# Recurrent attention phase of a two-layer kernel: the gate rows of chunk 0 made, stored and spread first, and the instruction orders of four engines written out per batch

## The chip, the cores and the metric

One core of one Trainium2 chip runs the whole program in one launch. The metric is the device time in microseconds (us) of a run, of which the median over some runs is given. The engines are called PE (matrix products), ACT (activations, copies with a scale), DVE (elementwise and scans), POOL (GpSimd) and SP (which issues DMAs).

## What is computed

The reference has two layers. The change concerns only the attention of layer 0, a gated recurrent attention (mLSTM) over 4 batches of 512 positions, 256 channels and 8 heads:

```python
logfg = jax.nn.log_sigmoid(f_pre)                 # gates, capped by 15 * tanh(x / 15)
Fcum = jnp.cumsum(logfg, axis=-1)
Dmat = Fcum[..., :, None] - Fcum[..., None, :] + i_pre[..., None, :]
Dmat = jnp.where(causal, Dmat, -jnp.inf)
m = jnp.max(Dmat, axis=-1, keepdims=True)
Smat = jnp.exp(Dmat - m)
C = qk * Smat
n = jnp.maximum(jnp.abs(jnp.sum(C, axis=-1, keepdims=True)), jnp.exp(-m))
h = jnp.einsum('bhst,bhtd->bhsd', C / n, v)
...
x1 = x + (jax.nn.sigmoid(o_pre) * h_norm) @ w_out
```

After it come the MLP of layer 0 with a mixture of low-rank experts, and layer 1 with softmax attention and a sparsified MLP. Those phases fill the time from about 140 us on.

## The kernel before

The attention phase is `mlstm_phase`. The 512 positions of a batch b are cut into C = 4 chunks of P = 128, so there are N = 16 chunks n = 4b + c. Every engine has its own list of instructions, executed in order, with semaphore waits between engines. A matrix product in full precision is three PE passes (`product`, lines 94 to 96) over operands split in a high and a low part: ACT copies the high part, DVE subtracts to get the low part.

**The gate rows.** After `gates(b)` has put the gate preactivations of all batches in one bank, ACT and DVE make rows of 32 x 512 (batch and head by position): ACT `Tanh`, `Exp`, `Tanh` and `Ln` (lines 745 to 750), DVE `gate_rows` (lines 1058 to 1078): a combination, a scan for the running sum `Fcum` (`F_SUM`, line 1068), a combination (line 1070), and a scan for the running maximum (`G_ROW`, line 1072). SP then stores the row in DRAM (`m_scratch`, line 361) and, for each chunk, loads it back spread over all 128 partitions (`spread_rows`, line 358) into one of a ring of six tiles `W`, 512 KB each. PE turns the gates (`turn_gates`, `TG_T`) and spreads sums (`spread_decay`), which ACT copies out or exponentiates (`tg`, `ends`, `ea`, and `eq` by `decay_of_queries`).

**A chunk n.** POOL masks W (`mask_weights`, line 849), ACT turns it to weights by eight `Exp` (`weights`, line 710), PE makes the scores (`score`, line 492) in banks 0 to 3, DVE multiplies scores and weights (`weigh_scores`, line 980, signals `PT_ready`), PE forms the weighted sum (`weighted`, lines 519 and 524) and the local state (`local_state`, line 507), DVE carries the state (`carry`), ACT evicts (`evict`, lines 717 and 718, "m_tot" and "m_sq"). `score(n)` waits for `weigh_scores(n - 1)`, since the banks are single.

**A batch b.** PE makes k, q, v and the output gate (`project_k`, `project_q`, `project_v`, `output_gate`) and ACT copies them out (lines 677, 682, 688, 693, 701). The results are normed in two halves f of two chunks: `mean_square`, `sum_squares` on DVE, `inverse_root` on POOL (line 863), `gate` and `norm` on DVE, `turn_h` on PE, `high_h` on ACT (line 731), `low_h` on DVE, `project_out` on PE, `add` on DVE. The order around the chunks is a loop `for b in range(B - 1)` with a body per engine, the same for b = 0, 1 and 2, and a written-out end for b = 3.

**The hand-over.** `following` is the opening of the next phase: squares of the result of batch 0 (`squares`, line 1317), their root on POOL, `scale_y` (line 1335), `turn_y` on PE, `high_y` and `low_y`, splits of the MLP weights (`split_high`, `split_low`), then `gates(pe, 0)` and `gates(pe, 1)`, the first two MLP units on PE, and `silu` and `hidden` for unit 0. Behind them the next phase puts its third unit on PE.

## Time and profile before

| | |
|---|---|
| median of 3 runs | 693.9 us (693.79 to 694.63) |
| the profiled execution's own time | 692.77 us |
| its span in the trace | 690.9 us |
| PE, DVE, ACT, POOL busy | 97%, 75%, 54%, 19% of the span |
| TensorE clock granted over the span | 0.998 of full |

A span is the time from the first to the last instruction of the trace; the execution's own time is 1.9 us more. Positions such as "at 40.17" are us from the start of the span. "Busy" of PE counts modelled ends of pipelined products, so a gap that the trace shows on PE is a lower bound of the time in which it had nothing to do.

### The profile page before, as it was taken

How to read it: one execution, taken by the hardware profiler on the slowest of the kernel's cores; microseconds unless marked ns; L12 is line 12 of the kernel's file. 1: busy time of each engine (PE TensorE's matmuls, PEld its weight loads, DVE VectorE, ACT ScalarE, POOL GpSimd, SP SyncE). 2: the span in 40 equal slices, each digit the busy share in tenths (PEclk: the TensorE clock that was granted, in tenths of full speed). 3: DMA queues.
4: the chain of work that ended last, by engine and by line, in shares of the span. 5: the costliest groups of instructions: out<-in, count | busy, mean ns of one | idle time of the engine just before them, and what ended most of it. 6: DMA issues, size and time to landing. Idle time of an engine off the chain costs nothing.

```text
span 690.9 us, 12153 instructions
## 1 busy us (share of the span) xinstructions
PE 666.7 (97%) x4808; PEld 560.5 (81%) x4808; DVE 518.5 (75%) x919; ACT 371.5 (54%) x775; POOL 129.3 (19%) x125
## 2 busy tenths in 40 slices
PE   7989998999999999999999999999899999999996
PEld 7867886878787888878888788887787889889886
DVE  7837879868856667565765676757679998989996
ACT  5887888747543444434443443446565454464541
POOL 7145445300000020000200002000133303203220
PEclk9999999999999999999999999999999999999999
DMA  5088442000210002000010100240000000000000
GB/s 198 5 264 313 108 146 71 1 1 1 63 29 4 1 1 64 1 31 1 1 64 0 32 1 1 93 183 2 0 1 1 0 17 16 1 31 1 1 31 31
DMA packets 24008, 31.27 MB, mean 45 GB/s; under 512 B 1232, under 2 KB 19952, under 8 KB 23184
## 3 DMA queue, kind: packets, MB, share of 16 engines
q1 hardware_dynamic: 23296, 29.18, 12.9%
q10 hardware_dynamic: 656, 1.31, 0.5%
q8 instruction: 38, 0.62, 0.4%
q14 instruction: 18, 0.15, 0.1%
HBM read 28.18 MB, written 2.31 MB: 44 GB/s over the span
## 4 chain that ended last, share of the span: by engine, by line
PE 62%; DVE 22%; ACT 9%; issue 3%; DMA 2%; POOL 1%; SPq 0%; DVEq 0%; ACTq 0%; POOLq 0%
PE bank L94 20%; PE bank L96 19%; PE bank L95 19%; ACT m_W L710 3%; DVE l_ring_lo L2551 3%; DVE l_ge L2532 2%; DVE l_h L2547 2%; DVE l_o L2555 1%; DVE h_raw L1227 1%; DVE l_h L2504 1%; DMA res<-in_x 1%; DVE h_ring_lo L1232 1%; DMA m_W<-m_scratch 1%; PE bank L519 1%; DVE l_oT_lo L2561 1%
## 5 line engine op out<-in xcount | busy, mean ns | idle before, releaser
L1227 DVE TENSOR_TENSOR h_raw<-h_s,bank 128x512 f32<-128x512 f32 x104 | 71.4, 686 | 107.1 <-ACT h_s L1217 92.7
L1217 ACT ACTIVATE h_s<-bank 128x512 f32<-128x512 f32 x104 | 62.2, 598 | 164.6 <-PE bank L96 164.5
L1232 DVE TENSOR_TENSOR h_ring_lo<-h_raw,h_ring_hi 128x512 fp32r<-128x512 f32 x92 | 68.9, 749 | 0.1
L1221 ACT ACTIVATE h_ring_hi<-h_raw 128x512 fp32r<-128x512 f32 x104 | 64.7, 623 | 2.0 <-DVE h_raw L1227 2.0
L95 PE MATMUL bank<-fused_lo,h_ring_hi 128*128 128x256 f32 x208 | 58.4, 281 | 0.0
L2251 ACT ACTIVATE l_s<-bank 128x512 f32<-128x512 f32 x32 | 19.1, 598 | 62.8 <-PE bank L96 62.6
L94 PE MATMUL bank<-l_xT_hi,l_wgu 128*128 128x512 f32 x128 | 51.2, 400 | 0.3
L94 PE MATMUL bank<-f_yT_hi,mlp_hi 128*128 128x512 f32 x128 | 50.6, 396 | 0.0
L95 PE MATMUL bank<-l_xT_lo,l_wgu 128*128 128x512 f32 x128 | 50.0, 391 | 0.0
L96 PE MATMUL bank<-l_xT_hi,l_lo 128*128 128x512 f32 x128 | 50.0, 390 | 0.0
L96 PE MATMUL bank<-f_yT_hi,fused_lo 128*128 128x512 f32 x128 | 50.0, 390 | 0.0
L95 PE MATMUL bank<-f_yT_lo,mlp_hi 128*128 128x512 f32 x128 | 49.9, 390 | 0.0
L94 PE MATMUL bank<-f_xT_hi,ffn_hi 128*128 128x512 f32 x104 | 41.5, 399 | 0.5 <-DVE h_raw L1227 0.5
L96 PE MATMUL bank<-f_xT_hi,fused_lo 128*128 128x512 f32 x104 | 40.7, 391 | 0.0
L95 PE MATMUL bank<-f_xT_lo,ffn_hi 128*128 128x512 f32 x104 | 40.6, 390 | 0.0
L95 PEld LDWEIGHTS bank<-fused_lo,h_ring_hi 128*128 128x128 f32 x208 | 39.2, 189 | 1.4
L710 ACT ACTIVATE m_W<-m_W,m_tg 128x128 f32<-128x128 f32 x128 | 39.2, 409 | 1.2 <-POOL m_W L849 1.2
L1729 POOL TENSOR_TENSOR late_rstd<-f_vv,minus_half 128x4 f32<-128x4 f32 x3 | 3.0, 1011 | 187.5 <-DVE f_vv L1878 187.5
L94 PE MATMUL bank<-l_wd,l_ring_hi 128*128 128x256 f32 x128 | 36.1, 282 | 1.6 <-DVE l_ring_lo L2551 1.6
L94 PE MATMUL bank<-mlp_hi,h_ring_hi 128*128 128x256 f32 x128 | 35.9, 281 | 0.7 <-DVE h_ring_lo L1232 0.7
L96 PE MATMUL bank<-mlp_hi,h_ring_lo 128*128 128x256 f32 x128 | 35.8, 280 | 0.0
L95 PE MATMUL bank<-l_lo,l_ring_hi 128*128 128x256 f32 x128 | 35.7, 279 | 0.0
(372 smaller groups left out, 1970.5 us busy)
## 6 DMA issues: line engine op xcount, KB each, us to landing
m_W<-m_scratch SPq DMA_DIRECT2D x16, 512.0 KB, 6.9
fused_raw<-in_fused SPq DMA_DIRECT2D x1, 3584.0 KB, 12.6
res<-in_x SPq DMA_DIRECT2D x4, 512.0 KB, 6.1
fused_raw<-in_fused SPq DMA_DIRECT2D x2, 1024.0 KB, 9.1
f_mask<-expert_weights SPq DMA_DIRECT2D x8, 256.0 KB
l_raw<-in_layer SPq DMA_DIRECT2D x1, 2048.0 KB, 8.9
out_x<-res SPq DMA_DIRECT2D x16, 128.0 KB, 1.9
f_xw<-in_turned_x SPq DMA_DIRECT2D x3, 512.0 KB, 5.7
```

The source lines that it names most:

```text
L94: nc.tensor.matmul(out, w[0], x[0], start=start, stop=False, skip_group_check=True)
L95: nc.tensor.matmul(out, w[0], x[1], start=False, stop=False, skip_group_check=True)
L96: return nc.tensor.matmul(out, w[1], x[0], start=False, stop=stop, skip_group_check=True)
L710: last = nc.scalar.activation(w[:, h, :], w[:, h, :], ACT.Exp, bias=tg[:, c, b * H + h:b * H + h + 1], scale=-1.0)
L1217: self.nc.scalar.activation(self.s[u % 2][r, :], gate[r, :], ACT.Silu).then_inc(self.silu.sem, 1)
L1221: self.nc.scalar.activation(self.unit(i, u)[0], self.product(i, u), ACT.Copy).then_inc(self.hi.sem, 1)
L1227: self.nc.vector.tensor_tensor(out=self.product(i, u), in0=self.s[u % 2][r, :], in1=up[r, :], op=ALU.mult).then_inc(self.hidden.sem, 1)
L1232: self.nc.vector.tensor_tensor(out=lo, in0=self.product(i, u), in1=f32(hi), op=ALU.subtract).then_inc(self.lo.sem, 1)
L2251: nc.scalar.activation(sb[u % 2][:, :], gate(u)[:, :], ACT.Silu).then_inc(silu.sem, 1)
L2532: nc.vector.tensor_tensor(out=ge[:, at:at + n, :], in0=ab[:, x, :].unsqueeze(1).to_broadcast([P, n, S]), in1=ab[:, x + 1:GP, :], op=ALU.is ...
L2547: nc.vector.scalar_tensor_tensor(out=x, in0=votes[:, j, :], scalar=least, in1=x, op0=how, op1=ALU.mult).then_inc(kept.sem, 1)
L2551: nc.vector.tensor_tensor(out=ring[j][1][:, :], in0=h[c][j][:, :], in1=f32(ring[j][0][:, :]), op=ALU.subtract).then_inc(lo.sem, 1)
```

## The change

**Gate rows in two parts.** `Ln`, the two combinations and the two scans run first on the 128 columns of chunk 0 and then on the other 384, the second scans starting from the last value of the first. SP stores chunk 0's part and spreads it at once; the rest is stored when `G_ROW` is there, and the other five tiles of the ring follow. In DRAM the rows lie as (chunk, row, position), so that a partition's 8 heads are one run of 4096 bytes where they were eight of 512. ACT also copies k of batch 0 between two of the row operations.

**Banks and waits.** The sums spread by PE go to banks 7, 4, 7, 4 and 4, so that banks 0 to 3 are free for `score(0)`, which now waits for `tg` and `x_rows` alone. ACT makes the weights of chunk 0 ahead of the decays.

**Orders written out.** The loops over b on PE, ACT, POOL and DVE become flat lists in which each batch has an order of its own; around the hand-over the squares and some splits stand elsewhere.

```diff
-    scratch = nc.dram_tensor("m_scratch", (R, S), fp32, kind="Internal").ap()
+    scratch = nc.dram_tensor("m_scratch", (C, R, P), fp32, kind="Internal").ap()
-    tg_bank, small_bank, spread_banks = bank[0], bank[1], [bank[2], bank[3], bank[4], bank[4]]
+    tg_bank, small_bank, spread_banks = bank[0], bank[4], [bank[7], bank[4], bank[7], bank[4]]
+    parts = slice(0, P), slice(P, S)
@@ sync
-            rows = scratch[of(b), chunk(c)].unsqueeze(0).to_broadcast([P, H, P])
-            sp.dma_start(W[n % RING][:, :, :], rows).then_inc(loaded[n % RING], 16)
-        sp.wait_ge(dve_rows, G_ROW)
-        sp.dma_start(scratch, row[5][0:R, :]).then_inc(stored, 16)
+            rows = scratch[c, of(b), :].rearrange("h s -> (h s)").unsqueeze(0).to_broadcast([P, H * P])
+            sp.dma_start(W[n % RING][:, :, :].rearrange("p h s -> p (h s)"), rows).then_inc(loaded[n % RING], 16)
+        sp.wait_ge(dve_rows, G_HEAD)
+        sp.dma_start(scratch[0], row[5][0:R, 0:P]).then_inc(stored, 16)
         sp.wait_ge(stored, 16)
         sp.wait_ge(gated, 1)
-        for n in range(RING):
+        spread_rows(0)
+        sp.wait_ge(dve_rows, G_ROW)
+        sp.dma_start(scratch[1:C].rearrange("c r s -> r c s"), row[5][0:R, P:S].rearrange("r (c s) -> r c s", s=P)).then_inc(stored, 16)
+        sp.wait_ge(stored, 32)
+        for n in range(1, RING):
             spread_rows(n)
@@ tensor
         def spread_decay(b):
-            if b == B - 1:
-                pe.wait_ge(eq_ready.sem, eq_ready.at(b - 1, 1))
+            if b == 0:
+                pe.wait_ge(og_in.sem, og_in.at(0, 2))
+            elif b == 1:
+                pe.wait_ge(act_tables, ENDS_IN)
+            else:
+                pe.wait_ge(eq_ready.sem, eq_ready.at(b - 2, 1))
@@ score(0)
-                pe.wait_ge(eq_ready.sem, eq_ready.at(1, 1))
-                pe.wait_ge(act_tables, ENDS_IN)
+                pe.wait_ge(act_tables, TG_IN)
+                pe.wait_ge(rows_in, 1)
@@ scalar
         nc.scalar.activation(row[1][f, :], row[0][f, :], ACT.Exp, scale=-CAP).then_inc(act_rows, 1)
+        copy_k(0)
         nc.scalar.activation(row[4][f, :], row[0][f, :], ACT.Tanh, scale=0.5 * CAP).then_inc(act_rows, 1)
         act.wait_ge(dve_rows, Y1)
-        nc.scalar.activation(row[3][f, :], row[2][f, :], ACT.Ln).then_inc(act_rows, 1)
+        for part in parts:
+            nc.scalar.activation(row[3][f, part], row[2][f, part], ACT.Ln).then_inc(act_rows, 1)
@@ vector, gate_rows
+            for p, ln, soft, f_sum, a_row, before in ((parts[0], LN_HEAD, SOFT1_HEAD, F_HEAD, A_HEAD, None),
+                                                      (parts[1], LN, SOFT1, F_SUM, A_ROW, slice(P - 1, P))):
...
+                nc.vector.tensor_tensor_scan(out=row[5][i, p], data0=gr[0:R, p], data1=gr[0:R, p], initial=row[5][i, before] if before else -3e38,
+                                             op0=ALU.max, op1=ALU.max).then_inc(dve_rows, 1)
@@ tensor, order of batch 0 (batches 1 to 3 have lists of their own)
+        local_state(0, 0)
+        score(1)
+        weighted(0, 0)
+        project_v(1, 0)
+        score(2)
+        weighted(0, 1)
+        project_v(1, 1)
+        local_state(0, 1)
+        score(3)
+        weighted(0, 2)
+        local_state(0, 2)
+        output_gate(1, 0)
+        score(4)
+        turn_h(0, 0)
+        output_gate(1, 1)
+        weighted(0, 3)
+        project_out(0, 0)
```

On DVE, in `gate_rows` from the `Ln` to the maximum, the kernel before has these rows (numbers behind the names are buffer numbers):

```order
L1066 SCALAR_TENSOR_TENSOR m_row_109<-m_row_109,m_row_111 32x512
L1068 SCALAR_TENSOR_TENSOR m_row_110<-ones_row,m_row_109 32x512
L1070 SCALAR_TENSOR_TENSOR m_gr<-m_row_108,m_row_110 32x512
L1072 SCALAR_TENSOR_TENSOR m_row_113<-m_gr 32x512
L1075 TENSOR_TENSOR m_qrow<-m_row_113 32x384
```

and the changed kernel these:

```order
L1151 SCALAR_TENSOR_TENSOR m_row_109<-m_row_109,m_row_111 32x128
L1153 SCALAR_TENSOR_TENSOR m_row_110<-ones_row,m_row_109 32x128
L1156 SCALAR_TENSOR_TENSOR m_gr<-m_row_108,m_row_110 32x128
L1158 SCALAR_TENSOR_TENSOR m_row_113<-m_gr 32x128
L1151 SCALAR_TENSOR_TENSOR m_row_109<-m_row_109,m_row_111 32x384
L1153 SCALAR_TENSOR_TENSOR m_row_110<-ones_row,m_row_110,m_row_109 32x384
L1156 SCALAR_TENSOR_TENSOR m_gr<-m_row_108,m_row_110 32x384
L1158 SCALAR_TENSOR_TENSOR m_row_113<-m_gr,m_row_113 32x384
```

Four rows of 512 columns became four of 128, after which chunk 0 can be stored, and four of 384.

On ACT, between the gate tables and the weights of chunk 1, the kernel before has these rows ("m_W_141" is the ring tile of chunk 0, "m_W_142" that of chunk 1):

```order
L769 ACTIVATE m_ea<-m_tg 128x128
L772 ACTIVATE m_eq<-bank 128x384
L776 ACTIVATE m_dexp<-m_dec 128x12
L772 ACTIVATE m_eq<-bank 128x384
L779 ACTIVATE m_ea<-m_ga 128x128
L772 ACTIVATE m_eq<-bank 128x384
L710 ACTIVATE m_W_141<-m_W_141,m_tg 128x128 x8
L677 ACTIVATE m_kT_105<-bank 128x512
L710 ACTIVATE m_W_142<-m_W_142,m_tg 128x128 x8
```

and the changed kernel these:

```order
L818 ACTIVATE m_ea<-m_tg 128x128
L753 ACTIVATE m_W_141<-m_W_141,m_tg 128x128 x8
L813 ACTIVATE m_eq<-bank 128x384
L720 ACTIVATE m_kT_105<-bank 128x512
L813 ACTIVATE m_eq<-bank 128x384
L824 ACTIVATE m_dexp<-m_dec 128x12
L826 ACTIVATE m_ea<-m_ga 128x128
L813 ACTIVATE m_eq<-bank 128x384
L753 ACTIVATE m_W_142<-m_W_142,m_tg 128x128 x8
```

The weights of chunk 0 moved ahead of five small operations, which now stand between the weights of chunks 0 and 1.

On ACT, at the end of the phase, the kernel before has these rows ("m_W_144" is the weights of chunk 15, "f_junk" the squares, "f_ys" is `scale_y`):

```order
L710 ACTIVATE m_W_144<-m_W_144,m_tg 128x128 x8
L717 ACTIVATE m_tot<-bank 128x264
L718 ACTIVATE m_sq<-bank 128x256
L1317 ACTIVATE f_junk_83,y_sq<-xn 128x256 x4
L731 ACTIVATE m_hT_hi<-bank,cols 128x256 x2
L140 ACTIVATE mlp_hi<-fused_raw 128x512 x2
L717 ACTIVATE m_tot<-bank 128x264
L718 ACTIVATE m_sq<-bank 128x256
L1335 ACTIVATE f_ys_82<-xn,y_rs 128x256 x4
```

and the changed kernel has the squares earlier, between two output gates of batch 3 ("m_th_145"):

```order
L744 ACTIVATE m_th_145<-bank 128x512
L1429 ACTIVATE f_junk_83,y_sq<-xn 128x256 x4
L774 ACTIVATE m_hT_hi<-bank,cols 128x256 x2
L744 ACTIVATE m_th_145<-bank 128x512
L760 ACTIVATE m_tot<-bank 128x264
L761 ACTIVATE m_sq<-bank 128x256
L753 ACTIVATE m_W_142<-m_W_142,m_tg 128x128 x8
```

The four squares moved from behind the weights of chunk 15 to ahead of those of chunk 13. Further on, `silu` of unit 0 ("h_s") moved behind the four copies "xn" and the last `high_h`, and two splits of MLP weights moved ahead of the last eviction.

## Rows read from the trace of the kernel before

**Rows 1.** The page: busy time, share of the span and instructions of each engine.

```profile
PE 666.7 (97%) x4808; PEld 560.5 (81%) x4808; DVE 518.5 (75%) x919; ACT 371.5 (54%) x775; POOL 129.3 (19%) x125
```

**Rows 2.** Stretches: length, then PE, PEld, DVE, ACT, POOL busy; clock, DMA share, GB/s.

```profile
40.00:60.00 20.00, 17.26 (x318) 13.40 (x322) 11.74 (x22) 18.10 (x58) 9.64 (x8) 1.00 0.95 326
60.00:68.00 8.00, 7.73 (x114) 5.46 (x105) 6.50 (x11) 4.77 (x15) 5.79 (x4) 1.00 0.83 272
68.00:90.00 22.00, 21.88 (x394) 17.92 (x394) 17.61 (x34) 17.47 (x54) 11.17 (x8) 1.00 0.43 118
90.00:112.00 22.00, 21.07 (x455) 17.05 (x457) 17.03 (x35) 19.40 (x61) 10.84 (x8) 1.00 0.45 146
112.00:124.50 12.50, 10.05 (x246) 7.20 (x241) 11.63 (x27) 11.09 (x35) 6.74 (x4) 1.00 0.01 3
124.50:140.00 15.50, 15.49 (x91) 13.76 (x92) 13.85 (x31) 12.64 (x26) 4.55 (x3) 1.00 0.01 2
```

**Rows 3.** The chain that ended last, 27 to 40 us: start, duration, what.

```profile
27.39 0.64 ACT m_row L750
...
28.12 0.69 DVE m_row L1066
...
28.84 1.22 DVE m_row L1068
...
32.04 1.63 DMA m_scratch<-m_row
...
33.68 5.22 DMA m_W<-m_scratch
...
39.05 1.10 POOL m_W L849
```

**Rows 4.** Timeline of ACT, 26 to 43 us: start, duration, instruction, [idle before, releaser].

```profile
26.09 1.28 ACT L750 ACT_TABLE_LOAD   x1
...
37.14 0.49 ACT L772 ACTIVATE m_eq<-bank 128x384 f32<-128x384 f32 x1 [0.26 <-PE bank L478]
...
40.17 2.45 ACT L710 ACTIVATE m_W<-m_W,m_tg 128x128 f32<-128x128 f32 x8 [1.25 <-POOL m_W L849]
```

**Rows 5.** Timeline of DVE, at 33 us.

```profile
33.33 0.28 DVE L1078 TENSOR_TENSOR m_diag<-ident,m_row 32x128 f32<-32x128 f32 x1
```

**Rows 6.** Line 351, the four loads of x, 4096 bytes per partition each.

```profile
DMA to landing us min/median/max: 4.0/6.1/8.8
```

**Rows 7.** Timeline of ACT, 57 to 68 us.

```profile
57.62 0.39 ACT L717 ACTIVATE m_tot<-bank 128x264 f32<-128x264 f32 x1 [0.52 <-PE bank L524]
...
59.49 0.60 ACT L701 ACTIVATE m_th<-bank 128x512 f32<-128x512 f32 x1 [1.20 <-PE bank L96]
...
61.27 0.39 ACT L717 ACTIVATE m_tot<-bank 128x264 f32<-128x264 f32 x1 [0.45 <-PE bank L524]
...
65.72 0.60 ACT L677 ACTIVATE m_kT<-bank 128x512 f32<-128x512 f32 x1 [1.46 <-PE bank L96]
...
67.64 1.27 ACT L682 ACTIVATE m_q<-bank,odd_even 128x512 f32<-128x512 f32 x2 [1.32 <-PE bank L96]
```

**Rows 8.** Timeline of ACT, 105 to 118 us.

```profile
105.06 0.60 ACT L701 ACTIVATE m_th<-bank 128x512 f32<-128x512 f32 x1 [1.21 <-PE bank L96]
...
106.83 0.39 ACT L717 ACTIVATE m_tot<-bank 128x264 f32<-128x264 f32 x1 [0.45 <-PE bank L524]
...
115.46 0.43 ACT L1317 ACTIVATE f_junk<-xn 128x256 f32<-128x256 f32 x1
...
117.51 0.82 ACT L731 ACTIVATE m_hT_hi<-bank,cols 128x256 fp32r<-128x256 f32 x2
```

**Rows 9.** Timeline of the hand-over: scale_y, silu of unit 0, third unit on PE.

```profile
119.80 1.71 ACT L1335 ACTIVATE f_ys<-xn,y_rs 128x256 f32<-128x256 f32 x4
...
127.54 0.60 ACT L1217 ACTIVATE h_s<-bank 128x512 f32<-128x512 f32 x1 [0.76 <-PE bank L96]
...
133.36 0.40 PE L94 MATMUL bank<-f_yT_hi,mlp_hi 128*128 128x512 f32 x1
```

More of the change, by code:

```diff
@@ new lines, in _ @@
+        score(7)
+        output_gate(2, 0)
+        weighted(1, 2)
+        output_gate(2, 1)
+        turn_h(1, 0)
+        weighted(1, 3)
+        score(8)
+        local_state(2, 0)
+        project_out(1, 0)
+        project_k(3)
+        score(9)
+        project_q(3)
+        weighted(2, 0)
+        score(10)
+        turn_k(3)
+        local_state(2, 1)
+        turn_h(1, 1)
+        weighted(2, 1)
+        project_v(3, 0)
+        project_v(3, 1)
+        weighted(2, 2)
+        local_state(2, 2)
@@ new lines, in _ @@
+        weights(6)
+        evict(1, 0)
+        high_h(0, 1)
+        copy_values(2, 0)
+        evict(1, 1)
+        weights(7)
+        copy_values(2, 1)
+        weights(8)
+        output_gate(2, 0)
+        evict(1, 2)
+        output_gate(2, 1)
+        high_h(1, 0)
+        evict(1, 3)
+        weights(9)
+        weights(10)
+        copy_k(3)
+        copy_q(3)
+        evict(2, 0)
+        copy_keys(3)
+        high_h(1, 1)
+        evict(2, 1)
+        weights(11)
+        copy_values(3, 0)
@@ L1133, in _ @@
[L1133 to L1151 removed]
+        weigh_scores(1)
@@ new lines, in _ @@
+        gate(0, 1)
+        weigh_q(2)
+        norm(0, 1)
+        carry(1, 0)
+        weigh_scores(5)
+        low_h(0, 1)
+        following.hid.credit_hidden(dve)
+        carry(1, 1)
+        mean_square(1, 0)
+        weigh_scores(6)
+        add(0, 1)
+        sum_squares(1, 0)
+        gate(1, 0)
+        weigh_scores(7)
+        carry(1, 2)
+        norm(1, 0)
+        normal_x(1)
+        low_h(1, 0)
+        mean_square(1, 1)
+        weigh_scores(8)
+        sum_squares(1, 1)
+        add(1, 0)
@@ new lines, in _ @@
+        gate(1, 1)
+        weigh_scores(9)
+        norm(1, 1)
+        carry(2, 0)
+        weigh_q(3)
+        normal_x(2)
+        low_h(1, 1)
+        weigh_scores(10)
+        mean_square(2, 0)
+        carry(2, 1)
+        gate(2, 0)
+        sum_squares(2, 0)
+        weigh_scores(11)
+        carry(2, 2)
+        norm(2, 0)
+        add(1, 1)
+        low_h(2, 0)
+        following.mean_square(dve)
+        weigh_scores(12)
+        mean_square(2, 1)
+        sum_squares(2, 1)
+        carry(3, 0)
```

396 lines of the change are left out of this document (193 added, 203 removed).

## The prediction

> **What bounds the kernel now.** I first read the busy line of the page [rows 1]: PE is busy 97% of the span, so over the whole program only a gap on PE can be won, and there are 690.9 - 666.7 = 24 us of them that the trace shows. Then I cut the span in stretches and looked for the gaps [rows 2]. From 124.5 to 140 us PE is busy 15.49 of 15.5 us: from the hand-over on, the rest of the program follows PE, and whatever is won before simply moves it forward. Ahead of it there are three kinds of stretch. From 40 to 60 us PE is short of work (17.26 of 20) while ACT is nearly full (18.10): ACT is the bound of batch 0. From 60 to 112 us PE is nearly full (7.73 of 8, 21.88 of 22, 21.07 of 22). From 112 to 124.5 us PE is short again (10.05 of 12.5), with ACT at 11.09 and DVE at 11.63. The PE gaps that the trace shows from 40 to 124.5 us add up to 2.74 + 0.27 + 0.12 + 0.93 + 2.45 = 6.5 us. The gaps are a lower bound, since the end of a product is modelled.
>
> Third, the chain that ended last shows what starts ACT's stretch [rows 3]: Ln, the combination, the scans, then the store of the gate row (1.63 us), the spreading load (5.22) and the mask on POOL (1.10), all in series, until ACT can make the first weights at 40.17. The timeline of ACT has 0.26 and 1.25 us of idle time just ahead of them [rows 4], and later, in the second half of batch 0, five waits for PE of 0.52, 1.20, 0.45, 1.46 and 1.32 us, 4.95 together [rows 7]. So ACT and PE take turns in waiting for each other.
>
> **Chunk 0 first.** ACT copies k ahead of the second Tanh, which puts about 0.5 us (0.60 in [rows 7], of which 0.1 overlaps) before the table load of 1.28 [rows 4]. Ln on 128 columns then starts at 27.4 + 0.5 = 27.9. Its price is not in the trace; it lies between a quarter of 0.64 [rows 3] and the 2.45 / 8 = 0.31 of an ACT operation with 128 columns [rows 4], and I take 0.3, as that has the same length: 28.2. On DVE two combinations of 128 columns cost 0.28 each [rows 5], and two scans, 1.22 for 512 columns [rows 3], between 0.28 and 0.31 by the column; I take 0.33 with overhead. With a gap of 0.03 us behind each that is 1.35 us, so chunk 0's row is ready at 29.6 instead of 32.0. The store takes 1.63 again: 31.2. The load has 128 runs of 4096 bytes instead of 1024 of 512. Its price is bounded by the 5.22 of before and by the 4.0 us of the fastest load of x, of the same size and the same runs [rows 6]. It lands between 35.2 and 36.4, and the mask and its start cost 1.2: W of chunk 0 is ready between 36.4 and 37.6.
>
> The Trainium skill's page "DMA: Bandwidth & Descriptors", section Specifications, gives 512 bytes as the smallest transfer at line rate, by which longer runs would win nothing and the load would stay at 5.22. By that the first weights start at 37.6, by the row of x at 36.9. I take 37.2, so this rule decides 0.4 us at most.
>
> The tables tg and ea are ready at about 36.9 as before (the operation ahead of the 37.14 row), for the longer part of the gate rows is split off: eight DVE instructions for four put the last scan some 0.6 us later, at 32.6, and what follows on PE waits for the second output gate anyway. So the first weights start near 37.2, 3 us earlier; but the 1.8 us of small ACT operations that filled 36.9 to 40.2 now stand behind them. The gain on ACT is the idle time alone: 1.51 less 0.3 = **1.2 us**. The other five spreads queue behind the second store, at about 34.3, 0.6 us later than the first one left before; the weights of chunk 1 are wanted only at 41.3, so this is hidden by the 4.1 us of ACT work ahead of them (2.3 of weights and the 1.8), as the load lands by 39.5 and the mask is done by 40.7. If the cover were gone, each us would count on ACT.
>
> **The order of batch 0.** The same instructions stand in another order, so the price is only in waits. Of the 4.95 us that ACT waits in [rows 7], the new lists put `high_h` and an eviction in front of the second output gate, which was the wait of 1.20, and score(0) and the projections no longer wait for the decays. Both engines must be free for a gain: PE shows 3.0 us of gaps from 40 to 68, ACT 1.5 + 4.95 = 6.5 us of waits. Going through the two new lists, I find one new wait of about 1 us, that of the last eviction of batch 0 for weighted(0, 3), which now stands behind the second output gate on PE; behind that eviction ACT has the gate copy and the weights of chunk 5. I take **3.5 us** for the head and batch 0 together, between 3.0 (the gaps shown) and 5.0 (half of the hidden part too).
>
> **Batches 1 and 2.** PE is nearly full; it shows 0.12 + 0.93 us of gaps from 68 to 112. I take **0.5 us**, between -0.5 (a wait more) and 2.
>
> **The end.** The squares take ACT 117.51 - 115.46 = 2.05 us [rows 8], in the middle of a stretch where ACT has no idle time from 106.83 on. They move to a place where ACT waited for PE 1.21 and 0.45 us [rows 8], which hides 1.7 of the 2.05. The end can follow only as far as DVE does: it is busy 11.63 of 12.5 us there [rows 2], but has 5 us free in the stretch ahead (17.03 of 22). I take **1.4 us**, between 0.5 and 2.4 (the gaps of PE).
>
> **The hand-over.** Silu of unit 0 came 127.54 - 119.80 = 7.7 us behind the start of `scale_y`, and PE's third unit, which needs its banks, 13.6 us behind [rows 9]. Now silu has more ahead of it. By the column, from 0.60 for 512, 1.71 for four times 256 and 0.82 for twice 256 [rows 7 to 9], I price scale_y at 1.7, the splits of 1536 columns at 1.5, high_y 1.2, the eviction 0.6, high_h 0.8, the four copies of x 1.7, the last two high_h 1.0, and the table load is 1.28: about 9.8 us, and with silu (0.5) and the product on DVE (0.6, a guess from the same 512 columns) 10.9. The slack is 2.7 us, so I count 0.2 for small waits of DVE, which is 13.85 of 15.5 us busy.
>
> The table load is 1.28 us in the row, and the copy behind it follows without more [rows 3, 4]. The Trainium skill's page "ScalarE: Activation LUTs", section What ACT_TABLE_LOAD costs, adds a drain of 1.38 for 2.66 together. By the page the slack would be 1.3 us; the sum is the same either way.
>
> The sum is 3.5 + 0.5 + 1.4 - 0.2 = 5.2 us: a span of 685.7, an own time of 692.8 - 5.2 = 687.6 us. The profiled execution was 1.1 below the median of its runs, so against that median I predict 693.9 - 5.2 = **688.7 us**.
>
> **The rivals.**
>
> *Only the head counts.* The middle is PE's and the end is DVE's: in 112 to 124.5 DVE leaves 0.9 us, and a batch that starts earlier only waits longer there. For it speaks the DVE row, against it that DVE is busy only 17.6 of 22 and 17.0 of 22 ahead, so it would be early as well. Then 1.2 of the head and 0.3 of the end remain: 692.4 us.
>
> *The hidden gaps go too.* PE's shown gaps are a lower bound, and ACT's waits are 6.5 us in the head alone. If the lists fit well, 4.7 us come in the head, 1.5 in the middle and 2.0 at the end: 8.2 less, 685.7 us. For it: no engine is full over 40 to 112 us but PE, whose busy time is overstated. Against it: fixed orders seldom hit both engines.
>
> *Order against the clock: slower.* In the new lists PE's output gates and v products stand directly ahead of a weighted sum or a score, and each waits for ACT to empty its bank. Where ACT is late, PE stops, and ACT then waits for PE: one round costs what such a wait costs now, 1.2 to 1.5 us [rows 7]. There are four such places a batch, twelve in all. The saving of 5.2 is gone with the fourth that newly bites; with six of the twelve the time is 6 x 1.35 - 5.2 = 2.9 above: 696.8 us. My walk through batch 0 found one.
>
> *The change does nothing.* The load of chunk 0 doesn't come earlier since 128 partitions read the same 4096 bytes, say 3 us more, and the small waits eat the rest: 693.9 us. The DMA engines are 0.95 busy from 40 to 60 us [rows 2] but idle before 34, so little speaks for it.
>
> **How the numbers follow.** A measurement of this kernel tells some 0.2%, or 1.4 us, from no change. Chances: forecast 0.55, with a range of its own from 686.5 to 691; only the head 0.15; hidden gaps 0.13; does nothing 0.08; slower 0.09. Only the head lies at the edge, a third of it within 0.2%. So faster 0.55 + 0.13 + 0.10 = 0.78, the same 0.13, slower 0.09. The range runs from 684.8, below the hidden gaps, to 693.5, beyond the head alone: it leaves out the slower case, half of no change and a little below, under 0.2 in all.
>
> **What would show it.** The first weights on ACT near 37.2 instead of 40.17, with the load of chunk 0 at 4.0 to 5.2 us. ACT without a gap of 1.2 us from there to the second output gate of batch 1. The weights of chunk 6, at 69.3 before by the ACT work behind the last of [rows 7], near 65.8. The squares ahead of the weights of chunk 13, and no ACT gap behind them. The first MLP product, at 124.5 before, near 119, and PE full from there; the third unit 8.9 us behind it. I am wrong if PE shows new waits on ACT's copies of v or the gates, if the third unit comes later than that by more than 0.5 us, or if the gain at 68 us has melted by 112.

## The result, and the profile after

The changed kernel takes 695.65 us (median of 12, 693.64 to 698.06), the kernel before beside it 693.76 (692.48 to 694.63): a ratio of 1.0026, with an interval from 1.0014 to 1.0039. It is slower by 0.26%, a small loss but clear of the interval, where 688.7 us were forecast with a range from 684.8 to 693.5. The profiled execution's own time is 695.59 us, its span 693.8, its granted clock 0.993 (before 692.77, 690.9 and 0.998).

The busy line of the page barely moved [rows 1]:

```profile
PE 668.6 (96%) x4808; PEld 561.5 (81%) x4808; DVE 521.5 (75%) x923; ACT 371.9 (54%) x776; POOL 130.1 (19%) x125
```

The stretches of [rows 2] in the kernel after (length, then PE, PEld, DVE, ACT, POOL busy, clock, DMA share, GB/s):

```profile
40.00:60.00 20.00, 16.99 (x273) 12.31 (x272) 9.04 (x17) 16.62 (x55) 9.32 (x7) 0.91 0.95 349
60.00:68.00 8.00, 7.91 (x120) 6.69 (x118) 6.91 (x13) 4.76 (x15) 3.40 (x3) 1.00 0.39 110
68.00:90.00 22.00, 20.92 (x387) 16.56 (x386) 18.26 (x34) 18.65 (x59) 12.01 (x7) 1.00 0.43 152
90.00:112.00 22.00, 21.89 (x396) 17.44 (x394) 17.08 (x35) 18.25 (x57) 11.50 (x7) 1.00 0.36 124
112.00:124.50 12.50, 10.59 (x308) 7.13 (x306) 11.87 (x29) 11.75 (x38) 6.52 (x3) 1.00 0.15 58
```

From 40 to 60 us PE has less work done than before at a clock of 0.91, and ACT, which was full, has 1.5 us less. Two places explain it. The first is the start of the program; the chain that ended last begins in the kernel after with

```profile
1.25 5.63 DMA gate_bias<-in_bias
...
6.90 0.15 DVE gate_bias L1169
...
7.04 1.32 DVE m_st L1024 x4
```

Here stands an edit that the forecast never priced and that the section on the change doesn't name: the line that scales `gate_bias` by 1/CAP, and its wait for two small loads, moved ahead of `statistics(0)`. In the kernel before the statistics start at 4.83 us; now they start at 7.0, and with them all that follows (the first gate product at 18.6 instead of 16.3). PE has nothing to do meanwhile, and the windows behind show its clock at the lower of its two levels, 1.2 GHz, for longer:

```profile
10.00:12.00 2.00, 0.00 (x0) 0.00 (x0) 1.93 (x12) 1.59 (x4) 1.18 (x3) 0.90 0.88 356
12.00:14.00 2.00, 1.46 (x7) 1.46 (x8) 1.93 (x12) 2.00 (x5) 1.15 (x3) 0.50 0.05 18
14.00:16.00 2.00, 1.93 (x10) 1.53 (x9) 1.93 (x11) 2.00 (x5) 1.14 (x3) 0.50 0.00 0
16.00:18.00 2.00, 2.00 (x11) 2.00 (x10) 1.98 (x3) 2.00 (x4) 1.92 (x4) 0.50 0.00 0
```

Before, the same windows have 1.00, 0.66, 0.50 and 0.98. The second place is in the chain near 50 us, inside `weighted(0, 1)`:

```profile
49.80 0.33 PE bank L527 x24
50.13 2.51 issue
52.64 0.78 PE bank L527 x40
```

and in the windows and the timeline of ACT around it:

```profile
50.00:52.00 2.00, 0.13 (x17) 0.02 (x3) 1.19 (x1) 1.25 (x5) 0.14 (x1) 1.00 1.05 442
52.00:54.00 2.00, 1.36 (x42) 1.20 (x43) 0.03 (x1) 0.00 (x0) 0.00 (x0) 0.64 1.07 459
54.00:56.00 2.00, 2.00 (x10) 1.90 (x9) 0.67 (x2) 1.37 (x5) 0.00 (x0) 0.51 0.84 363
```

```profile
54.63 0.39 ACT L760 ACTIVATE m_tot<-bank 128x264 f32<-128x264 f32 x1 [3.38 <-PE bank L532]
...
61.74 0.60 ACT L744 ACTIVATE m_th<-bank 128x512 f32<-128x512 f32 x1 [1.24 <-PE bank L96]
```

PE stops behind product 24 of 64 without waiting for any data ("issue"), then runs some 3 us at about half its clock, and ACT waits 3.38 us for it. The rest is as the change meant it. The SP timeline and the first weights:

```profile
32.11 0.34 SPq L363 DMA_DIRECT2D m_scratch<-m_row  x1
34.02 0.34 SPq L360 DMA_DIRECT2D m_W<-m_scratch  x1
...
37.75 2.48 SPq L360 DMA_DIRECT2D m_W<-m_scratch  x5
...
43.81 0.36 SPq L112 DMA_DIRECT2D fused_raw<-in_fused  x1
```

```profile
39.11 2.44 ACT L753 ACTIVATE m_W<-m_W,m_tg 128x128 f32<-128x128 f32 x8
```

The load of chunk 0 takes 3.7 us from its issue to the mask at 37.71 (5.4 before, [rows 3]). The last row of SP is new too: five spreads are issued in 2.48 us, so the first load of the fused weights, 3.5 MB, starts at 43.81, where the kernel before starts it at 46.92.

The signs that the forecast named came out like this. The first weights on ACT start at 39.11 us (forecast 37.2), those of chunk 6 at 71.89 (65.8), the first MLP product at 127.94 (119), and the third unit 9.0 us behind that (8.9).

All versions have the same number of products behind them at the weights of chunk 9 (977), at those of chunk 15 (1467) and at the first MLP product (1704), so the span can be cut there. The cuts, from the timelines of DVE, ACT and PE, in us:

| | before | after | e4 |
|---|---|---|---|
| start to the first statistics | 4.83 | 6.97 | 4.92 |
| to the weights of chunk 0 | 35.34 | 32.14 | 32.07 |
| to the weights of chunk 9 | 44.71 | 48.73 | 45.07 |
| to the weights of chunk 15 | 27.71 | 28.95 | 28.97 |
| to the first MLP product | 11.92 | 11.15 | 10.69 |
| to the end | 566.34 | 565.89 | 565.69 |
| span | 690.85 | 693.83 | 687.41 |

(Version e4 is the changed kernel with two edits undone, below. The traces of before and of e4 are of executions about 1 us faster than their medians, that of after is not.) Against before, the changed kernel gains 3.2 us in the head, 0.8 at the end and 0.4 behind it, and pays 2.1 at the start, 4.0 in batch 0 and 1.2 in batches 1 and 2.

Executions of one kernel differ by their mean granted clock: of 145 of the kernel before, 75 had 0.997 or more and a median of 693.0 us, the others 694.7, and below "at a full clock" is the median of the first kind.

### The profile page after: what moved, and what is told of

It reads as the page before. It is cut to its first block, busy times and chain, and to the rows that moved or that the text cites. A ratio compares the mean times of both kernels' runs of the same rounds, so it can differ in the third digit from the quotient of the medians.

```text
span 693.8 us, 12159 instructions
## 1 busy us (share of the span) xinstructions
PE 668.6 (96%) x4808; PEld 561.5 (81%) x4808; DVE 521.5 (75%) x923; ACT 371.9 (54%) x776; POOL 130.1 (19%) x125
## 4 chain that ended last, share of the span: by engine, by line
PE 70%; DVE 20%; ACT 5%; issue 3%; POOL 1%; DMA 1%; ACTq 0%; DVEq 0%
PE bank L94 22%; PE bank L96 20%; PE bank L95 20%; DVE l_ring_lo L2663 3%; DVE l_ge L2644 2%; DVE l_h L2659 2%; DVE l_o L2667 1%; PE bank L527 1%; DVE l_h L2616 1%; PE bank L500 1%; DVE h_raw L1339 1%; PE bank L532 1%; DVE xn L1128 1%; DMA gate_bias<-in_bias 1%; PE bank L515 1%
```

## The experiments

Medians are of 12 executions, of 6 for e4 and e15, 11 for e9. A ratio is to the kernel before on the same chip. The experiments ran on five chips (e1 to e4; e5 to e8; e9 to e12; e13 to e15; e16 and e17), on which the kernel before had medians from 693.24 to 694.15 us, so a difference of medians across chips is uncertain by some 0.9 us. Figures at a full clock compare only a part of the executions, and the part differs from kernel to kernel, so both are given where they disagree. Each version has one trace.

**e1: the bias line back.** On DVE:

```diff
-        dve.wait_ge(cols_loaded, 32)
-        nc.vector.tensor_scalar(out=gate_bias15..., scalar1=1.0 / CAP, ...)
         for b in range(B):
             statistics(b)
+        dve.wait_ge(cols_loaded, 32)
+        nc.vector.tensor_scalar(out=gate_bias15..., scalar1=1.0 / CAP, ...)
```

> The changed kernel with one line put back: DVE scales the gate bias behind the statistics of x, as in the kernel before, and not ahead of them. Theory A (DVE waits at that line for the small load of the bias, which lands at 6.9 us, while x is there at 4.8; all that follows is 2.0 to 2.3 us late): the first statistics start at 4.8 instead of 7.0, the first gate product on PE at 16.3 instead of 18.6, and the median falls by 2.0 us against the changed kernel, to about 693.7. Rival (the start is hidden, since PE waits for the projection weights or the store of the gate rows anyway): less than 0.5 us. If the stop of PE at 50 us hangs on where the big load of weights meets PE's code, it may move as well.

**e2: the kernel before with the bias line at the front** (the same edit the other way round).

> The kernel before with that one line moved to the front of DVE, as the changed kernel has it. Theory A: 2.0 us slower than the kernel before, about 695.8, with the first statistics at 7.0. Rival: below 0.5 us slower.

e1 took 693.03 us, 2.6 less than the changed kernel, ratio 0.9981 (0.9964 to 0.9998); e2 696.31, ratio 1.0032 (1.0018 to 1.0046), 2.2 more than the kernel before there. Its chain starts with the same wait (5.89 us of "DMA gate_bias<-in_bias"). None of the 12 executions of the changed kernel and none of e2 had a full clock, 7 of 12 of e1. So the line costs 2.2 to 2.6 us. The rest of the change wins 1.1 us over the kernel before there, and not 5: the stop is there in e1 too, 3.06 us at 48.6.

**e3: the load in small pieces.** e1, with the first fused load as seven of 1024 columns (4096 bytes a partition instead of 28,672):

```diff
-[[(g.fused_raw[:, a:b], fused_in[:, a:b])] for a, b in zip(cuts, cuts[1:])]
+the first group as [(g.fused_raw[:, n:n + 1024], fused_in[:, n:n + 1024]) for n in range(a, b, 1024)]
```

> As the kernel with the bias line put back, and the first load of fused weights (3584 KB in rows of 28672 bytes) cut into seven loads of 4096 bytes per partition. Theory B (PE stopped for 2.5 us at 50 us in the middle of a weighted sum because its next block of code waited on a DMA engine behind packets of 28672 bytes, 1.06 us each; the stop then halved the TensorE clock for some 3 us): with packets of 4096 bytes the stop shrinks to under 0.5 us, the granted clock stays at 1.0 from 50 to 58 us, and the time falls by 2.5 to 4 us against the kernel with the bias line put back. Rival C (PE waits there for something of its own, a semaphore or a bank, that the trace does not name): the stop stays at 2.5 us at the same instruction.

693.36 us, ratio 0.9984 (0.9969 to 1.0), and a stop of 2.23 us at the same product. The theory expected under 0.5 us; the size of the load's pieces isn't the cause.

**e4: the load later.** e1, with

```diff
-        after.issue(sp, 0)
         for n in range(RING, N):
             spread_rows(n)
+            if n == 7:
+                after.issue(sp, 0)
```

> As the kernel with the bias line put back, and the first load of fused weights issued behind the spreading load of chunk 7 instead of ahead of that of chunk 6, some 5 to 8 us later. Theory B: no stop in the weighted sum at about 48 to 50 us, but the code blocks that PE fetches every 6 us can meet the load later, so a stop of 1 to 2.5 us may show elsewhere; 0 to 4 us faster than with the bias line alone. Rival C: the stop stays at the same instruction, and the time changes by less than 0.5 us.

690.09 us, ratio 0.9932 (0.9918 to 0.9947). The stop is gone, the windows from 46 to 58 us are all at 1.00. It is 4.1 us faster than the kernel before there, at the upper end of what was expected. As **e15** it ran again on another chip, as the measure for e13 and e14:

> The kernel of e4 once more, as the measure for e13 and e14 on their chip: 690.0 to 690.4 us at a full clock, ratio to before between 0.993 and 0.996. If its six executions were a lucky sample the ratio is above 0.997.

689.94 us, 0.9947 (0.9933 to 0.9961). The gain holds.

**e5: the same edit in the kernel before; e9: the same edit in the changed kernel** with its bias line still at the front.

> The kernel before with one edit: its first load of the fused weights is issued behind the spread of chunk 7 instead of ahead of that of chunk 6. The trace of the kernel before has no stop of PE near 50 us. Theory (the late load in e4 won because it no longer lies ahead of PE's instruction block): there is nothing to win here, so within 0.1% of before, 693.5 to 694.9, first MLP unit within 0.5 us of 124.5. Rival (a late load is worth its 4 us by itself, since chunk loads or splits come sooner): 690 to 691, ratio near 0.994.

> The changed kernel with one edit: the first load of the fused weights is issued behind the spread of chunk 7; the line of gate_bias15 stays at the very front of DVE. If the two causes of the loss add up (e1 gained 2.6 us by the bias line, e4 another 2.9 by the load), this gives back the second alone: 695.65 - 2.9 = 692.7 on the scale of the first comparison, about 1 us under before, ratio near 0.9985. The first gate product stays late, near 18.6, and the stop of PE near 50 us is gone. Rival (they share one cause, the late start shifts the block into the load): over 694.5, or under 691 if the late start costs nothing by itself.

e5: 692.12 us, 0.9973 (0.9957 to 0.999). Neither "nothing" nor "4 us": at a full clock it is 1.0 under before (692.04 against 693.05), since the spreads of chunks 6 and 7 go ahead of the 3.5 MB; the weights of chunk 6 start 1.1 us earlier. So of what e4 wins over e1, 2.1 us at a full clock, up to 1 is this. e9: 692.29 us, near the 692.7 expected, 3.4 under the changed kernel and 2.2 above e4. Its ratio is 1.0001 (0.9985 to 1.0018) where 0.9985 was expected; from the changed kernel's 1.0026 that is 0.0025, or 1.7 us, with 4.8 left to e4's 0.9932. The two causes together are the whole difference between the changed kernel and e4 (5.6 us by medians, 6.5 by ratios), and each costs something with the other gone (e1 and e9 against e4). How it divides between them is known only within these figures: 1.7 to 3.4 us for the load, 2.2 to 4.8 for the line.

**e12: the load between; e10: runs of 512 bytes; e17: two of seven pieces early; e16: six more products.** Four edits of e1 that ask what PE's stop is. e12 puts `sp.wait_ge(intra.sem, 1)` ahead of the load. e10 takes the rows' layout of before, eight runs of 512 bytes. e17 issues two of e3's seven pieces at the old place and five behind chunk 7. e16:

```diff
         turn_y(1)
-        idle_products(6)
+        idle_products(12)
```

> Version e1 with SP waiting for the first weighted sum (intra 1) ahead of the first load of the fused weights, which is then issued near 46 us instead of 42, still ahead of the spreads of chunks 6 and 7. PE passes the place at which the kernel before fetched its second instruction block near 42.3 us. Theory (the block is held up by a bulk load that was issued ahead of it, and by nothing else of the load): the block is in before the load starts, the stop is gone, and the time is near e4's: 690.3 to 691. Rival (it is the amount of bulk traffic that PE's stop follows, or e4 won because chunk 6 is no longer behind the load): the stop stays or chunk 6 is late, 692.5 to 693.5.

> Version e1 (the changed kernel with the bias line back behind the statistics) with the gate rows stored as before, (row, position), so that a spread reads and writes eight runs of 512 bytes per partition where e1 has one of 4096; chunk 0 is still stored and spread first. Theory: the load of chunk 0 takes 5.2 us to the mask's start instead of 3.7, so the first weights start 1.5 us later than e1's 37.61 (near 39.1), and the stop of PE near 49 us is still there, since PE's block waits behind bulk transfers whatever the size of their packets: 694.5. Rival (it is the spreads' 4096-byte packets that hold PE's block back, and with 512 bytes it comes through in 0.75 us as in the kernel before): the stop is gone and the time is near 691.5.

> Version e1 with the first load of the fused weights in seven pieces of 1024 columns as in e3, two of them (1 MB) at the old place ahead of the spread of chunk 6 and five behind the spread of chunk 7. Theory (the block waits for the bulk bytes queued ahead of it, 3.5 MB in e1): the stop shrinks to under 1 us or is gone, and the time is near e4's, 690.0 to 690.8. Rival (any part of the load there holds the block up for its whole wait): a stop of over 2 us, 692.5 or more.

> Version e1 (changed kernel, bias line back behind the statistics) with twelve idle products instead of six at the start of PE, where it waits anyway: six more instructions, which the trace counts as twelve matmuls. Theory (PE runs dry at the end of a block of its program, at a fixed number of instructions): the stop near 48 us is there again and comes behind product 12 of 64 of the weighted sum instead of product 24, 692.5 to 693.5 us. Rival (PE waits for data of that weighted sum, or the stop is set by time): it stays behind product 24, or at the same time with the count unrelated.

The timelines of PE at the stop, first e1 and e17, then e12, e10 and e16 (in each the second row is the one behind the stop):

```profile
48.20 0.40 PE L527 MATMUL bank<-m_v,m_W 128*32 128x33 f32 x24
51.66 0.78 PE L527 MATMUL bank<-m_v,m_W 128*32 128x33 f32 x40 [3.06 <-issue]
```

```profile
48.82 0.40 PE L530 MATMUL bank<-m_v,m_W 128*32 128x33 f32 x24
51.58 0.56 PE L530 MATMUL bank<-m_v,m_W 128*32 128x33 f32 x40 [2.37 <-issue]
```

```profile
51.38 0.75 PE L528 MATMUL bank<-m_v,m_W 128*32 128x33 f32 x62
53.79 0.22 PE L528 MATMUL bank<-m_v,m_W 128*32 128x33 f32 x2 [1.66 <-issue]
```

```profile
54.26 0.75 PE L527 MATMUL bank<-m_v,m_W 128*32 128x33 f32 x62
56.54 0.22 PE L527 MATMUL bank<-m_v,m_W 128*32 128x33 f32 x2 [1.53 <-issue]
```

```profile
51.40 0.65 PE L527 MATMUL bank<-m_v,m_W 128*32 128x33 f32 x50
52.69 0.33 PE L527 MATMUL bank<-m_v,m_W 128*32 128x33 f32 x14 [0.65 <-issue]
```

PE stops at one of two places: behind product 24 of `weighted(0, 1)` in the changed kernel, e1, e3 and e17, behind product 62 of `weighted(0, 2)` in e12 and e10. With twelve more matmuls at its start it is product 50, exactly twelve earlier. Counted from the start of PE's program, that is behind matmul 346 at the first place and behind matmul 472 at the second, in e16 too. So the stop goes by the place in PE's list, not by data and not by time. (My expectation had it at the first place; the second block came in time there.) Which of the two places it is goes by which packet of the program is late: that for the first place ran in time in e10, e12 and e16 (37.90, 45.21 and 38.62 us). When the fused load is issued doesn't decide it alone, since e16 issues it at 41.63, ahead of e1's 42.28. The views of the DMA queues show what is late: queue q8, "instruction", moves 38 packets of 16 KB in a run, one for every 126.5 of PE's 4808 matmuls, and the two places are 126 matmuls apart. From this I take it that each packet is a block of PE's program. In the changed kernel none from 44 to 50 us and one from 50 to 51:

```profile
q1 hardware_dynamic: 477, 2.52, 107.0%
```

```profile
q1 hardware_dynamic: 15, 0.43, 99.6%
q8 instruction: 1, 0.02, 5.9%
```

In the kernel before that packet runs at 42.25 us, with 223 of PE's matmuls started, in e4 at 40.72, with 216; in the changed kernel at 50.20 and in e1 at 49.23, with 346 started and PE dry. e12, whose load is issued 3.1 us later than e1's (45.41 and 42.28), gets it at 45.21 and is late with the next one, 51.55. In all seven traces with such a stop (changed, e1, e3, e10, e12, e16, e17) PE goes on 1.3 to 1.6 us behind the end of the packet. The times: e12 692.1 us, ratio 0.9989 (0.9971 to 1.0007), profiled span 687.8; e10 694.27, 1.0012 (0.9997 to 1.0028); e17 693.45, 0.9986 (0.9965 to 1.0008); e16 691.17, 0.9971 (0.9954 to 0.9988). e12 too missed its expectation of 690.3 to 691: the first block came in time, the second didn't. e17 goes against what I expected: 1 MB ahead of the block is enough for a stop of 2.4 us. So it isn't the load's size in proportion. Without any part of it ahead, in e7, e9, e11 and e15, the packet still ran only at 46.4, 48.4, 46.1 and 45.8 us, behind the spreads of chunks 1 to 5, and PE, with 306 to 308 matmuls started, stopped for 0.5 us at most. e15 is the kernel of e4, where it ran at 40.7: the time of that packet moves by 5 us between two executions of one kernel, and what more stands in the queue takes the slack that is left. A stop seen in one trace need not be in every execution, and the fastest execution of e1 took 689.85 us. e10's stop is the shorter one at the second place and not, as expected, the one near 49 us. Its first weights start 33.4 us behind the first statistics, 1.0 later than in e1: that is what the longer runs are worth.

**e6: one store.** e4 with the gate rows whole again, and all spreads behind one store:

```diff
-        sp.wait_ge(dve_rows, G_HEAD)
-        sp.dma_start(scratch[0], row[5][0:R, 0:P]).then_inc(stored, 16)
-        ...
-        spread_rows(0)
         sp.wait_ge(dve_rows, G_ROW)
```

> Version e4 with the gate rows whole again: Ln, combinations and scans on 512 columns, one store, then all six spreads; layout, banks and orders stay. It is what chunk 0 first is worth where nothing disturbs it. By the prediction's head term (idle time of ACT alone) it costs 1.2 us: 691.3, and the first weights start about 2.4 us later, near 39.4, than e4's 37.00, with the five small ACT operations that stand behind them waiting too. Theory: as ACT's list has the weights ahead of those operations, all of the delay counts on ACT, so 2 to 2.5 us: 692.3. Rival (PE bounds batch 0 and takes the delay up): under 0.5 us, 690.5.

693.87 us, 0.9996 (0.9981 to 1.0012). At a full clock (3 of 12 executions) 693.2, 3.3 above e4: more than the theory's 2.5 and far more than the forecast's 1.2. In the trace the first weights are 2.2 us later behind the first statistics (34.26 against 32.07), and 1.4 more are lost by the weights of chunk 9. There PE is busy for only 2.04 of the 4 us from 40 on and its clock is at 0.50 from 44 to 46. So 2.2 is what chunk 0 first is worth at the first weights; how much of the rest is the clock's wasn't separated.

**e8 and e14: chunk 0 first alone.** The kernel before with the rows in two parts, two stores, the new layout and the late load, all orders as before.

> The kernel before with chunk 0 first alone: gate rows in two parts, two stores, rows of 4096 bytes per partition; the orders of all engines, the banks and the loop over batches as before, and the first load of the fused weights behind the spread of chunk 7, so that it can't meet PE's block. The small ACT operations stand ahead of the first weights, as before. By the prediction's head term ACT's idle of 1.51 us ahead of the weights shrinks by 1.2: 692.8 if batch 0 passes it on. Theory (the gain of e4 over before comes from the orders together with the early chunk 0, not from the early chunk alone): 693 to 694. Rival (the head alone is worth the 3 us by which chunk 0 is early): 691.

> The kernel of e8 once more (chunk 0 first alone, the load late, orders of before). Its executions at a full clock took 690.7 to 692.2 us. If the early chunk 0 passes through on its own, the weights of chunk 6 start near 67.5 (69.28 before, 68.17 in e5) and the first MLP unit near 122.7, 1.2 us under e5: median 691.0. Rival: the gain at chunk 6 has melted by chunk 15, and the first unit is at 123.9 as in e5.

692.15 us, 0.998 (0.996 to 0.9999), and again 692.8, 0.9983 (0.9968 to 0.9997). Over all executions that is no gain on e5 (692.12, 0.9973). At a full clock, which 9 of the 24 executions had and 8 of 12 of e5, it is 690.9 both times, 1.1 under e5. The trace of e14 has the weights of chunk 6 at 67.4 (e5 68.2), those of chunk 15 at 110.67 (e5 111.47) and the first MLP product at 122.6 (e5 123.9). So 0.8 us pass through to chunk 15. The other 0.5 is e5's own: its clock is at 0.88 from 112 to 126 us, and it takes 12.44 us from the weights of chunk 15 to that product, where before, e2, e8 and e14 take 11.92. The trace of e8 itself was of its slowest execution (695.21 us), at half its clock from 40 to 48 us, and settles nothing. Whether the early chunk alone wins 0.8 to 1.1 us or, with the lower clock that more of its executions have, nothing, stays open.

**e7: the squares back** behind the weights and evictions of chunk 15, on ACT, and their mean on DVE.

```diff
         evict(3, 1)
+        following.squares(act)
         following.split_high(act, 0, 2)
```

> Version e4 with the four squares of the result of batch 0 back behind the weights and evictions of chunk 15 on ACT, and their mean on DVE back behind the first mean square of batch 3, as in the kernel before. By the prediction's end term it costs 1.4 us (0.5 to 2.4): 691.5, with the first MLP unit that much later than e4's 121.73. Rival (DVE bounds the end, so ACT's 1.8 us of squares lie beside it): 690.1 to 690.5.

692.75 us, 0.9994 (0.9974 to 1.0014). From the weights of chunk 15 to the first MLP product it takes 12.3 us, e4 10.7: 1.6 us for the squares in the trace. The difference at a full clock is 2.8, on another chip than e4; the traces have the rest ahead of the weights of chunk 9 (0.7) and behind the MLP product (0.3), where the edit changes nothing.

**e11 and e13: the loss in batch 2.** In the changed kernel DVE's `normal_x(1)` is slow, and PE waits for the `low_h` behind it. The rows of DVE, POOL and PE:

```profile
85.13 3.66 DVE L1128 TENSOR_SCALAR xn<-res,moment,roots 128x256 f32<-128x256 f32 x4
88.71 0.86 DVE L1123 SCALAR_TENSOR_TENSOR m_hT_lo<-bank,cols,m_hT_hi 128x256 fp32r<-128x256 f32 x2
```

```profile
85.36 1.12 POOL L919 TENSOR_SCALAR_AFFINE_SELECT m_W<-m_W 128x1024 f32<-128x1024 f32 x1 [1.12 <-DVE m_hh L1116]
86.46 1.09 POOL L926 TENSOR_TENSOR m_ktil<-m_ktok,m_ea 128x512 f32<-128x512 f32 x1
87.50 1.14 POOL L919 TENSOR_SCALAR_AFFINE_SELECT m_W<-m_W 128x1024 f32<-128x1024 f32 x1
```

```profile
89.63 0.39 PE L94 MATMUL bank<-wo_hi,m_hT_hi 128*128 128x256 f32 x1 [1.08 <-DVE m_hT_lo L1123]
```

e11 puts `normal_x(1)` behind `weigh_scores(8)`; e13 puts lists of PE, ACT and DVE from the middle of batch 1 to the middle of batch 2 back in the order of before.

> Version e4 with one edit on DVE: normal_x(1) stands behind weigh_scores(8) instead of ahead of low_h(1, 0). In e4 its four instructions on 128x256 took 3.66 us together, one of them 1.18, beside POOL's mask and scaling at 79.6 to 82.9 us; in the kernel before the same four take 1.38 to 1.4 us everywhere. low_h(1, 0) then ended late and PE waited 1.08 us for it ahead of project_out(1, 0) at 83.84. Theory (DVE's instruction is slowed by POOL beside it, and that wait is the loss of batches 1 and 2): the four take 1.4 us again, the wait on PE is gone, the chunk-10 to chunk-15 landmarks come 1.1 us earlier, 689.0. Rival (the wait only moves to the next hand-over between DVE and PE): 690.0, within 0.3 us of e4.

> Version e4 with the stretch from the middle of batch 1 to the middle of batch 2 in the order of the kernel before: on PE project_out(1, 0), score(9), project_k(3), project_q(3), turn_k(3), weighted(2, 0), score(10), local_state(2, 0); on ACT k, q and keys of batch 3 ahead of the weights of chunk 10; on DVE normal_x ahead of the gates and norm ahead of carry. Theory (the new lists of batch 2 lose 1.3 us between the weights of chunks 9 and 13, 23.76 us in e4 against 22.50 before): 22.5 us again there, and 688.8 us, 1.3 under e4 on the same chip. Rival (the loss is the price of batch 3's new start, which stays, and only moves to the next wait): within 0.4 us of e4.

Each of the three slow instructions of `normal_x(1)` (1.18, 1.14 and 1.17 us; the first takes 0.41) ends 0.14 to 0.15 us behind the end of one of POOL's. Not every instruction of POOL does this: in the kernel before the same four lie wholly beside POOL's `inverse_root` (3.00 us on 128x16) and take 1.38 together.

e11: 690.38 us, 0.996 (0.9942 to 0.9977), no better than e4, by its rival. The four instructions take 1.37 us and the wait of 1.08 is gone, but PE now waits 0.8 us for `add` and 0.8 for the state. e13: 691.4 us over ten executions (two more took over 2,200 us), 0.997 (0.9951 to 0.9989), at a full clock 690.0 as e4. From the weights of chunk 9 to those of chunk 13 it takes 23.6 us (e4 23.8, before 22.5). Its theory fell as well: with that stretch in the old order two waits of 0.6 us (one each for DVE and ACT) stand where one of 1.1 was. POOL's list and the rest of batch 2 kept the new order.

Batch 0 has the same pair, and no version takes it out. In e4 `normal_x(0)` starts beside POOL's scaling and mask, and PE waits for the `low_h` behind it:

```profile
56.27 2.89 DVE L1129 TENSOR_SCALAR xn<-res,moment,roots 128x256 f32<-128x256 f32 x4
60.00 0.39 PE L94 MATMUL bank<-wo_hi,m_hT_hi 128*128 128x256 f32 x1 [1.25 <-DVE m_hT_lo L1124]
```

## Why the prediction was wrong

Four steps failed. The sum has no term for the bias line and none for the load that SP issues sooner; the term for the order of batch 0 was too large; and that for batches 1 and 2 had the wrong sign.

**Head and batch 0, 3.5 us.** In the kernel as it is, the stretch from the start to the weights of chunk 9 costs 3.0 us instead of winning 3.5. Most of that are the two things left out, below. The rest is a wrong size. The first weights start 3.2 us sooner behind the statistics (forecast: 3.0), and at 36.99 us in e4 (forecast 37.2), so the sum for the head was right. The size of the rest can be read, by one trace each, where the two things are away. From the first statistics to the weights of chunk 9 before takes 80.05 us, e5 78.81, e14 78.07 and e4 77.14. Of e4's 2.9 us, 1.2 are thus the late load alone, which the forecast doesn't have; chunk 0 first makes 0.7 (forecast 1.2), and the orders, with the small ACT operations behind the first weights, 0.9 (forecast 2.3). The change itself is worth 1.7 us here and not 3.5, outside its bounds of 3.0 to 5.0. "The idle time alone" is nearly right for chunk 0 with the old orders; with ACT's new order the same early chunk is worth 2.2 or more (e6), since the small operations stand behind it. The one new wait that the walk through the lists found, "about 1 us" for `weighted(0, 3)`, is 1.92 us on ACT in e4 (at 58.78), and the wait of 1.25 on PE at 60.00 it didn't find. One premise of the walk is wrong as well: in the diff `project_q(1)` does wait for a decay, that of batch 2 (`eq_ready.at(B - 2, 1)`), where before it waited for an output gate.

**What was left out: the bias line.** The wait for `cols_loaded` was moved ahead of `statistics` on DVE, and the working, which put nothing at the start, said of no step what is queued behind it. It cost 2.2 to 2.6 us by medians (e1, e2, e9 against e4).

**What was left out: what SP does sooner.** The working priced the five spreads and not the load behind them. SP issues them in 2.5 us where six took 10.3, so the 3.5 MB start 3.1 us earlier and stand ahead of a block of PE's program. The stop of 2.51 us, the halved clock behind it and ACT's wait cost 3.4 us by medians and 1.7 by ratios (e9 against the changed kernel; 2.9 and 3.4 in e4 against e1), of which up to 1 is the gain that a late load has anyway (e5). The Trainium skill's page "Runtime: NRT & Kernel Launch", section Instruction fetch mechanics, says that each engine refills its instructions in blocks of 16 KiB over a queue of its own and that this is mostly hidden. The packets of q8 agree on the size. That it is hidden holds for e4, which has no stop, and not for the seven traces with one.

**Batches 1 and 2, -0.5 us.** Wrong in sign, and beyond its bound of 0.5 for "a wait more": 1.2 us lost between the weights of chunks 9 and 15 in all versions with the new lists. In the changed kernel 1.08 of it is one wait of PE. The page "GPSIMD Engine Reference" of the Trainium skill, section Specifications, says that POOL shares its SBUF interfaces with DVE, and that they contend when the DVE instruction is in a two-port mode or has two inputs in SBUF. The rows agree that they contend (1.18 against 0.41 us for one TENSOR_SCALAR, only beside POOL's mask or scaling); in which mode it ran no row shows. But e11 and e13 show that this wait isn't the cause of the loss, since others take its place. Which order would keep the 1.2 us stays open.

**The end, -1.4 us.** Right: 1.2 in e4 (0.8 in the changed kernel), and 1.6 come back with the squares (e7). The squares lie at 107.06 to 109.2 us, where the rows gave them room.

**The hand-over, +0.2.** Size off, with the other sign: silu is 12.1 us behind `scale_y` (134.93 and 122.84; forecast 9.8) and still in time. The third unit is 9.0 us behind the first (forecast 8.9), and the fourth to fifth take 6.7 us instead of 7.5, so this part won 0.4 to 0.7.

**The table load and the 512 bytes.** The table load is 1.28 us in both, and the next instruction starts right behind it (133.63 and 134.93 in the changed kernel). The Trainium skill's drain of 1.38 us ("ScalarE: Activation LUTs", What ACT_TABLE_LOAD costs) isn't in these rows. Of the load of chunk 0 the row was nearer than the page: runs of 4096 bytes are 1.0 us faster (e10). The Trainium skill's "DMA: Bandwidth & Descriptors", section Specifications, has 512 bytes as the smallest transfer at line rate; the reading that longer runs therefore win nothing didn't hold.

**The sum.** With the bias line and the stop away, what is left of the 5.2 us is 1.7 in the head and batch 0, -1.2 in batches 1 and 2, 1.2 at the end and 0.7 behind it, together about 2.3. The medians of e5 and e4, which both have the late load, differ by 2.0. So even without the two things left out the time would have stayed some 3 us above the forecast.

**The rivals.** "Order against the clock" gave the sign and, by luck, nearly the time (696.8): there is no wait on the copies of v or the gates of 1.35 us in six places, but one line, one block of program and one wait. "Only the head counts" is what e8 is, 1.1 us at a full clock and nothing over all executions, plus the late load's 1.0. Of the signs of being wrong, the last one showed in e4 too: its lead of 3.2 us at the weights of chunk 6 (66.10 against 69.28) is 1.6 at those of chunk 15.

## What to carry to other kernels

Go through the full diff engine by engine, and price for every moved wait what is queued behind it; here one moved line, absent from every sum, cost 2.2 us or more. When a queue gets faster, ask what it starts sooner: here a bulk load came ahead of a block of PE's program. If PE stops on "issue" in the middle of a group, look at the instruction queue in that window, move the bulk load by a few us, and check the clock behind it. The best version is e4: 690.0 us over its 12 executions, 0.53 to 0.68% faster than before, of which a late load in the kernel before has 0.27% (e5).

## What was unexpected of the hardware

- A block of PE's program can come late behind bulk loads: its packet ran at 40.72 and 45.82 us in two executions of the same kernel without a stop, and at 49.23 in e1 and 50.20 in the changed kernel, with stops of 3.06 and 2.51 us. The packets of 16 KB themselves take 0.9 us. Behind the stops of 2.23 us and more (e3, e17, changed, e1) the rows show PE's clock down to 0.50 to 0.52; behind those of 1.66 (e12), 1.53 (e10) and 0.65 (e16) it stays at 1.00.
- How often a kernel runs at its full clock isn't chance alone: 11 of 12 executions of e4's kernel had it, 75 of 145 of before, none of 24 with the bias line at the front of DVE and the early load (the changed kernel and e2), 2 of 11 of e9. What decides it was not tried.
- Four DVE instructions take 3.66 us beside POOL's mask and scaling, 1.37 alone, and 1.38 beside POOL's `inverse_root` on 128x16.
